# A two-layer kernel on one core: seven half-size sums on GpSimd, new landing places for x1, and another order in the second span

## What is computed

```python
def _L0_cond_ref(x, language_ids, W, Wr, A, B):
    base = jnp.einsum('btd,od->bto', x, W)
    logits = jnp.einsum('btd,ed->bte', x, Wr)          # 8 experts
    logits = logits + one_hot(language_ids) * 5.0
    topw, topi = jax.lax.top_k(logits, 2)
    weights = jax.nn.softmax(topw, axis=-1)
    gates = jnp.sum(one_hot(topi) * weights[..., None], axis=-2)
    h = jnp.einsum('btd,erd->bter', x, A)              # rank 16
    lora_out = jnp.einsum('bter,bte,eor->bto', h, gates, B)
    return base + 2.0 * lora_out

x = x + _L0_cond_ref(x, itok_B_0_7, L0_cond_W, L0_cond_Wr, L0_cond_A, L0_cond_B)
x = x + jnp.einsum('bsi,boi->bso', x, L1_cond_weight[itok_B_0_15])
```

## Time and profile before

| | us |
|---|---|
| median of 3 runs | 419.42 |
| lowest and highest | 417.97, 420.1 |
| the profiled execution | 418.74 |
| its span, first to last instruction | 416.7 |
| TensorE busy | 398.2 (96%) |
| VectorE busy | 315.4 (76%) |
| ScalarE busy | 170.9 (41%) |
| GpSimd busy | 56.6 (14%) |

### The profile page before, as it was taken

How to read it: one execution, slowest core, us unless ns; L and a number is a source line. 1 busy time by engine, 2 the same in 40 slices (tenths; PEclk the granted TensorE clock), 3 DMA queues, 4 the chain that set the end, 5 groups by cost and what they waited for, 6 DMA issues and landing times.

```text
span 416.7 us, 5965 instructions
## 1 busy us (share of the span) xinstructions
PE 398.2 (96%) x1920; PEld 333.2 (80%) x1920; DVE 315.4 (76%) x412; ACT 170.9 (41%) x231; POOL 56.6 (14%) x80
## 2 busy tenths in 40 slices
PE   8999989899999989999999997999998999999996
PEld 8989868688889868788888885878786887878784
DVE  2899999997454148929887489979797979899700
ACT  2342242664220141434353255555455564555511
POOL 1010100000000000000100025241231415142000
PEclk9999999999999999999999999999999999999999
DMA  8977510133476200007693999999999999999231
GB/s 189 218 212 194 152 53 0 51 102 101 127 216 207 57 0 2 1 1 204 138 302 106 329 232 263 282 257 293 280 263 281 254 304 258 284 264 295 62 102 50
DMA packets 78578, 72.79 MB, mean 175 GB/s; under 512 B 7091, under 2 KB 77267, under 8 KB 77523
## 3 DMA queue, kind: packets, MB, share of 16 engines
q1 hardware_dynamic: 51584, 47.21, 44.6%
q10 hardware_dynamic: 26962, 25.21, 19.4%
HBM read 55.61 MB, written 16.78 MB: 174 GB/s over the span
## 4 chain that ended last, share of the span: by engine, by line
PE 39%; DVE 33%; issue 14%; ACT 4%; DMA 4%; SPq 3%; ACTq 1%; POOL 1%; DVEq 0%
PE banks L1058 8%; PE banks L1060 8%; PE banks L1059 8%; DVE weights L612 7%; DVE weights_f L606 5%; DVE tokens L596 4%; DVE turned_w L612 4%; PE banks L1051 4%; SPq L371 3%; PE banks L1155 3%; PE banks L1156 3%; PE banks L1157 3%; DVE weights L462 2%; ACT tokens L916 2%; DVE turned_w_f L450 2%
## 5 line engine op out<-in xcount | busy, mean ns | idle before, releaser
L1058 PE MATMUL banks<-ring,weights 128*128 128x512 f32 x192 | 75.4, 393 | 5.2 <-DVE weights L462 1.7
L418 POOL TENSOR_TENSOR raw<-raw,ident 128x128 f32<-128x128 f32 x50 | 38.2, 764 | 269.2 <-DMA raw<-in_L_cond_weight_dram 230.1
L1155 PE MATMUL banks<-weights,tokens 128*128 128x512 f32 x176 | 68.9, 392 | 3.1 <-DVE tokens L596 3.1
L1156 PE MATMUL banks<-weights,tokens 128*128 128x512 f32 x176 | 68.5, 389 | 0.0
L1157 PE MATMUL banks<-weights,tokens 128*128 128x512 f32 x176 | 68.5, 389 | 0.0
L926 ACT ACTIVATE weights<-weights_f 128x1024 fp32r<-128x1024 f32 x44 | 46.6, 1062 | 52.9 <-DVE weights_f L606 51.2
L606 DVE STREAM_TRANSPOSE weights_f<-raw 128x1024 f32<-128x1024 f32 x42 | 51.7, 1232 | 1.4 <-POOL raw L418 0.8
L612 DVE TENSOR_TENSOR weights<-weights_f,weights 128x1024 fp32r<-128x1024 f32 x44 | 52.1, 1186 | 0.4 <-ACT weights L926 0.4
L1060 PE MATMUL banks<-ring,turned_w 128*128 128x512 f32 x128 | 49.8, 389 | 0.0
L1059 PE MATMUL banks<-tokens,weights 128*128 128x512 f32 x128 | 49.8, 389 | 0.0
L1058 PEld LDWEIGHTS banks<-ring,weights 128*128 128x128 f32 x192 | 36.0, 188 | 14.2 <-issue 3.2
(11 more groups left out here) (109 smaller groups left out, 626.6 us busy)
## 6 DMA issues: line engine op xcount, KB each, us to landing
raw<-in_L_cond_weight_dram SPq DMA_DIRECT2D x168, 128.0 KB, 3.6
ring_f<-in_L_cond_weight_dram SPq DMA_DIRECT2D x88, 128.0 KB, 6.2
raw<-in_x_dram SPq DMA_DIRECT2D x64, 128.0 KB, 3.3
x_kept<-stage ACTq DMA_DIRECT2D x32, 256.0 KB, 4.2
tokens_f<-x_kept ACTq DMA_DIRECT2D x8, 1024.0 KB, 8.3
out_dram<-sums ACTq DMA_DIRECT2D x32, 256.0 KB, 5.1
raw<-in_L_cond_W_dram SPq DMA_DIRECT2D x32, 128.0 KB, 3.0
raw<-in_L_cond_A_dram SPq DMA_DIRECT2D x4, 128.0 KB, 2.9
```

The source lines that it names most:

```text
L418: nc.gpsimd.tensor_tensor(spot, spot, ident[:].rearrange("p (q j) -> p q j", q=Q), ALU.add)\
L1058: nc.tensor.matmul(ps, u_hi, x_hi, start=first and k == 0, stop=False, skip_group_check=True)
L1155: nc.tensor.matmul(l1_bank(o), x_hi, w_hi, start=m == 0, stop=False)
L1156: nc.tensor.matmul(l1_bank(o), x_hi, w_lo, start=False, stop=False)
```

## The change

- In the first span the four T1, the first three S4 and the four S1 move from VectorE to GpSimd's list, between and behind its `add_ones`. T1(t) for t > 0 waits for T2(t - 1), S4(r) for S2(r), S1 for the end of the gates. VectorE makes S4(3) itself, after three S4 of GpSimd.
- In the second span `copy_h` and `exponentials` come ahead of the high parts for product 2 on ScalarE, and the gates and T3 ahead of its low parts on VectorE.
- In both spans TensorE turns the gated h after two k steps of product 7, before after three.
- x1 of rows 2 and up lands in `stage` (even rows) and `sums2` (odd rows). Row 3's load stands behind `high_w1(8)`, row 2's behind output 0, row r + 3's behind the first output of row r for r of 1 to 4; `x1_high(row + 2)` stands behind a row's last output, and `x1_low(row)` from row 2 on behind `low_w1` when n % 8 is 2. Row 1's stay.

The diff, with most of the unchanged lines around it cut:

```diff
@@ -351,6 +351,12 @@
+        def x1_landed(row):
+            if row < 2:
+                return x1_place(row, 1, tokens_f)
+            return stage[:] if row % 2 == 0 else sums2[:].rearrange("p (s a) f -> p s (a f)", s=2)
         def x1_part(row, low):
@@ -420,8 +426,40 @@
                 add_ones(("w", m))
+            def make_t1(t):
+                pool.wait_ge(featured, featured_at(0, 0, t) + 1)
+                if t == 0:
+                    pool.wait_ge(lo_done, PIECE_AT["wt", HM - 1] + 1)
+                else:
+                    pool.wait_ge(t2_done, t)
+                pool.wait_ge(transposed, TURN_AT[x_item(0, 1, t)] + 1)
+                nc.gpsimd.tensor_tensor(half_x(0, t, 0), half_x(1, t, 0), half_x(0, t, 0), ALU.subtract)\
+                    .then_inc(t1_done, 1)
+            def make_s4(r):
+                pool.wait_ge(s2_done, r + 1)
+                a12 = quarter_w(3, r)
+                nc.gpsimd.tensor_tensor(a12, a12, s2_sum(r), ALU.subtract).then_inc(s4_done, 1)
+            def make_s1(r):
+                pool.wait_ge(gate_steps, GATE_STEPS)
+                a21, a22 = quarter_w(5, r), quarter_w(4, r)
+                nc.gpsimd.tensor_tensor(a21, a21, a22, ALU.add).then_inc(s1_done, 1)
+            make_t1(0)
+            make_t1(1)
+            add_ones(("w", HM))
+            make_t1(2)
+            add_ones(("w", HM + 1))
+            make_t1(3)
+            add_ones(("w", HM + 2))
+            make_s4(0)
+            add_ones(("w", HM + 3))
+            make_s4(1)
+            make_s4(2)
             for r in range(HM):
-                add_ones(("w", HM + r))
+                make_s1(r)
             for n in range(NW1):
@@ -501,12 +539,6 @@
                     .then_inc(bd_summed, 1)
-
-            def make_s1(r):
-                dve.wait_ge(s3_done, r + 1)
-                dve.wait_ge(s2_done, r + 1)
-                a21, a22 = quarter_w(5, r), quarter_w(4, r)
-                nc.vector.tensor_tensor(a21, a21, a22, ALU.add).then_inc(s1_done, 1)
@@ -593,7 +625,7 @@
                     dve.wait_ge(x1_hi_done, 2 * row + j + 1)
-                    nc.vector.tensor_tensor(x1_place(row, 1)[:, j], x1_place(row, 1, tokens_f)[:, j],
+                    nc.vector.tensor_tensor(x1_place(row, 1)[:, j], x1_landed(row)[:, j],
                                             x1_place(row, 0)[:, j].bitcast(F32), ALU.subtract).then_inc(x1_ready, 1)
@@ -641,18 +673,14 @@
             low(("wt", 3))
-            make_t1(0, 0)
             turn(x_item(0, 1, 1))
             make_t2(0, 0)
-            make_t1(0, 1)
             turn(x_item(0, 1, 2))
             make_t2(0, 1)
-            make_t1(0, 2)
             turn(x_item(0, 1, 3))
             make_t2(0, 2)
-            make_t1(0, 3)
             turn(("w", 4))
@@ -676,22 +704,16 @@
             lows("u", 7)
-            for r in range(HM):
-                make_s4(r)
+            dve.wait_ge(s4_done, 3)
+            make_s4(3)
             lows("x", 0, 7)
             make_gates(0)
-            add_p1(0, 0)
-            add_p1(0, 1)
+            for r in range(HM):
+                add_p1(0, r)
             turn(("b",))
-            make_s1(0)
             low(("b",))
-            add_p1(0, 2)
-            add_p1(0, 3)
-            make_s1(1)
-            make_s1(2)
             gT_low(0)
-            make_s1(3)
@@ -747,24 +769,21 @@
             low(("x", 1, 1, 3))
-            lows("x", 1, 2)
             for t in range(XT):
                 make_t1(1, t)
+            make_gates(1)
+            for t in range(XT):
+                make_t3(1, t)
+            lows("x", 1, 2)
             for k in range(HM):
             low(("x", 1, 6, 3))
-            for t in range(XT):
-                make_t3(1, t)
             for r in range(HM):
                 add_p1(1, r)
-            low(("x", 1, 7, 0))
-            make_gates(1)
-            low(("x", 1, 7, 1))
-            low(("x", 1, 7, 2))
-            low(("x", 1, 7, 3))
+            lows("x", 1, 7)
             gT_low(1)
@@ -776,7 +795,9 @@
                 low_w1(n - 1)
-                if n % M == 5:
+                if n == M + 5:
+                    x1_low(1)
+                elif n > M + 5 and n % M == 2:
                     x1_low(n // M)
@@ -903,17 +924,21 @@
                     act.wait_ge(steps, product_end(1, 3))
-                else:
-                    act.wait_ge(l1_ready, (row - 1) * 2 * TT)
+                elif row == 3:
+                    act.wait_ge(summed_up, added_at(1, "12", HM - 1) + 1)
+                elif row >= 4:
+                    act.wait_ge(x1_ready, 2 * (row - 1))
                 for slot in range(KEPT):
-                    act.wait_ge(kept[slot], (HM if row < NB // 2 else 2 * HM) * 16)
-                act.dma_start(x1_place(row, 1, tokens_f).rearrange("p s f -> p (s f)"),
+                    act.wait_ge(kept[slot], (HM if row in (0, 1, 3) else 2 * HM) * 16)
+                act.dma_start(x1_landed(row).rearrange("p s f -> p (s f)"),
                               x1_kept[row].rearrange("p m t -> p (m t)")).then_inc(x1_loaded[row % 2], 16)
                 act.wait_ge(x1_loaded[row % 2], (row // 2 + 1) * 16)
+                if row >= 2:
+                    act.wait_ge(l1_ready, (row - 1) * 2 * TT)
                 for j in range(2):
-                    nc.scalar.activation(x1_place(row, 0)[:, j], x1_place(row, 1, tokens_f)[:, j],
+                    nc.scalar.activation(x1_place(row, 0)[:, j], x1_landed(row)[:, j],
                                          ACT.Copy).then_inc(x1_hi_done, 1)
@@ -1000,17 +1025,14 @@
             keep_all(0, "12")
-            highs("x", 1, 2)
             copy_h(1, 0)
             copy_h(1, 1)
+            exponentials(1)
+            highs("x", 1, 2)
             for r in range(HM):
             highs("x", 1, 6)
-            high(("x", 1, 7, 0))
-            exponentials(1)
-            high(("x", 1, 7, 1))
-            high(("x", 1, 7, 2))
-            high(("x", 1, 7, 3))
+            highs("x", 1, 7)
             for r in range(HM):
@@ -1018,6 +1040,7 @@
             high_w1(8)
+            load_x1(3)
             high_w1(9)
@@ -1025,10 +1048,14 @@
                 row, last = o // (2 * TT), o % (2 * TT)
-                if last == 1 and row + 1 < NB:
-                    x1_high(row + 1)
-                if last == 2 * TT - 1 and row + 2 < NB:
-                    load_x1(row + 2)
+                if o == 0:
+                    load_x1(2)
+                elif o == 1:
+                    x1_high(1)
+                elif last == 0 and row + 3 < NB:
+                    load_x1(row + 3)
+                elif last == 2 * TT - 1 and row + 2 < NB:
+                    x1_high(row + 2)
             for s in range(OUTS):
@@ -1105,9 +1132,9 @@
                 product(s, 6, lambda r: pe.wait_ge(p1_copied, HM * s + r + 1), False, main_bank)
-                product(s, 7, lambda r: pe.wait_ge(u2_copied, HM * s + r + 1), False, main_bank, range(HM - 1))
+                product(s, 7, lambda r: pe.wait_ge(u2_copied, HM * s + r + 1), False, main_bank, range(2))
                 turn_gated(s)
-                product(s, 7, None, False, main_bank, range(HM - 1, HM))
+                product(s, 7, None, False, main_bank, range(2, HM))
                 pe.wait_ge(gT_done, s + 1)
```

## The result

The changed kernel takes **414.31 us** (median of 4 runs, 413.56 to 414.8), the kernel before 419.36 beside it (4 runs); ratio 0.988, 95% interval 0.985 to 0.991. The forecast was 411.6, with a range of 407.3 to 416.6. The profiled execution took 414.6 us, its span is 412.8.

The account below looks back on a forecast made before the run. TensorE, busy 96% of 416.7 us, was taken as the bound, so only its idle time could be won. Spans -4.0, rows 2 to 7 -6.9, row 1 +3.6 sum to -7.3: 411.4 from 418.74, stated as 411.6, range 407.3 to 416.6.

Parts of the forecast that it names:

- product 6 later: First span: T1 saved on VectorE are given back as waiting, so product 6 starts 0.7 us later.
- the spans' four other waits: Both spans: TensorE's waits for gT_low, quarter 11's first addition, copy_h and copies of U2 go; -4.7 us.
- row 1's wait: Second layer, row 1: early x1 loads in row 0 delay W1 tiles 11 to 13; +3.6 us, ends 0 and +8.
- rows 2 to 7: Second layer: x1's high part made a row earlier lets VectorE catch up; all six waits go, -6.9 us.
- T1 was put at 1.4 us: First span: one 128x512 sum on GpSimd takes 1.4 us, between 0.46 and 1.84.
- The rival that these sums grow to over 2.4 us: First span: GpSimd's sums hold VectorE's second operand, product 6 about 11 us later, 423 in all; chance 0.07.
- the forecast 41.9: First span: T1(3) stands behind the ones of W piece 5, so T2(3) starts near 41.9 instead of 41.20.
- forecast a wait of 5 to 6.5 us: Sign of being right: TensorE waits 5 to 6.5 us at the start of row 1.
- its times for tiles 11 and 13, 245.0 and 249.6: Row 0: row 3's x1 load costs 4.8 us of W1 traffic, so tiles 11 and 13 land at 245.0 and 249.6.
- that it would be idle in every later row: Second layer, sign of being right: VectorE stands idle in each row after row 1.
- The rival that the weights' stream sets the rows: Rows 2 to 4: W1 stream sets them, or second load hits row 1; +2 to +5, 413.6 to 416.6; chance 0.20.
- 0.27 us: Amount added to each TensorE wait's idle time, taken from row 1's start, as its full cost.

Follow-up runs that it names:

- with the load moved away: Changed kernel with row 3's x1 load moved from behind high_w1(8) to behind row 0's last output; 411.0 us, ratio 0.979.
- the version with x1 early: Changed kernel with T1(2), T1(3) ahead of the ones, row 3's load behind row 0's last output, x1_high(1), x1_low(1) behind tile 9; 408.2 us.
- the ten with 48 fillers: Ten executions of the changed kernel with 48 unused identity matmuls on TensorE ahead of row 1's wait; median 416.8 us.

## Why the prediction was right, and where its sum was short

| term | predicted | measured |
|---|---|---|
| product 6 later | +0.7 | +1.06 (55.00 to 56.06) |
| clock behind product 6 | not in the sum | +1.6 |
| the spans' four other waits | -4.7 | -5.0 |
| row 1's wait | +3.6 | +3.3 |
| clock behind row 1 | not in the sum | +2.1 |
| rows 2 to 7 | -6.9 | -6.9 |

Measured is between the two profiled executions. The spans' term is what is left when the first two are taken from row 0's start, 226.72 instead of 229.00. That of rows 2 to 7 is 132.68 us from row 1's start to row 7's (254.44 to 387.12) against 137.48 before, -4.8, without the 2.1 of the clock. From -2.3, +3.3 and -4.8 follow -3.8, and the spans differ by 3.9.

**GpSimd's sums.** T1 was put at 1.4 us and took 1.27 to 1.30; beside a VectorE step with two operands S4 took 1.68, against 1.30 beside a transpose. In reverse, VectorE's low part and T2 beside T1(3) and the ones behind it took 1.06 and 0.94, where 0.65 and 0.69 is usual. This is the lock between a VectorE step with two SBUF inputs and a GpSimd instruction that reads SBUF, as the Trainium skill's "SBUF — State Buffer", section "Who interferes with whom", states it, and these rows agree. The rival that these sums grow to over 2.4 us is out. That T1(2) and T1(3) would stand behind the ones was foreseen, and T2(3) at 41.95, 0.75 us later than before, is the forecast 41.9 almost exactly. The other 0.3 us up to product 6 are lost behind it, where T2(3) took 0.94 us instead of 0.68.

**The first span behind product 6 and the second span.** The steps came within a microsecond of what was written, and all four waits went. gT_low ran from 77.26 to 78.48 and was done before lora, at 80.43; the four S1 ran from 70.74 to 75.79.

**Row 1.** The mechanism and the size were right: forecast a wait of 5 to 6.5 us, measured 5.80. The working has two faults. The load cost the stream 3.2 us and not 4.8. And the prediction took its times for tiles 11 and 13, 245.0 and 249.6, from a kernel whose spans were not yet shorter, while its sum has row 1's delay behind the spans' gain: with the load moved away tile 13 landed at 242.72, 2.0 us earlier than before, with the spans. So tile 13 landed at 245.98, not 249.6, and VectorE turned it at 247.48, not 250.1. By the prediction's own times a TensorE 4 us ahead would have waited some 10 us; the forecast of 5 to 6.5 comes from the 3.6 of the sum. The rest is ScalarE's: the high part of tile 13, an output and two halves of x1's high part follow one another from 248.75 to 252.9, and x1_low(1) stands 2.20 us waiting for it:

```profile
250.94 2.00 ACT L941 ACTIVATE tokens<-tokens_f 128x1024 fp32r<-128x1024 f32 x2 [0.65 <-ACT sums L962]
252.03 2.36 DVE L628 TENSOR_TENSOR tokens<-tokens_f,tokens 128x1024 fp32r<-128x1024 f32 x2 [2.20 <-ACT tokens L941]
```

From tile 13's landing to row 1's start it is 8.46 us (245.98 to 254.44), before 8.67 (244.76 to 253.43). The wait is this chain against a TensorE that arrives 2.3 us earlier and a tile that arrives 1.2 us later, 3.2 for the load less 2.0 for the spans.

**Rows 2 to 7.** All six waits went, as forecast, and rows 2 to 6 take 21.76 us each. Their cause was the one named: VectorE's own waits behind row 1's start, first before, then now (total us, times, longest):

```profile
DVE tokens L596 <- ACT tokens L916: 13.1, 6, 2.2
```

```profile
DVE weights_f L638 <- POOL raw L424: 3.0, 4, 1.9
DVE weights_f L638 <- POOL ring_f L424: 1.9, 3, 0.9
```

The wait for ScalarE's high part of x1 is gone, and VectorE waits 4.9 us for tiles instead, which TensorE doesn't feel. In rows 2 to 5 VectorE was busy for 19.50 to 21.40 us of 21.76; that it would be idle in every later row did not hold in row 6, where it was busy throughout and still in time. (The 1.4 us of waits for tiles that the prediction took from the page were those of 42 of the 64 tiles; the other 22 had 5.3 us, but none of it behind row 1's start.) The rival that the weights' stream sets the rows did not come here, since TensorE came late to row 1. With row 1 started at 254.44 the tiles cost nothing later, nor at 251.38 with the load moved; at 248.22 they cost a wait of 1.1 us, at 245.1, with no wait at row 1, 4.0 to 4.3. So the limit was real, and it takes most of what is won by repairing row 1 once product 6 is repaired.

**What was missing.** The sum priced a wait at its idle time and 0.27 us, from a row in which the clock held. It had no term for the clock, though it made one wait longer by 3.3 us and another by over 1. Those 1.6 + 2.1 us, with small differences of the other terms, are the whole way from 411.4 to 414.6. The range held them only by what it kept for the weights' stream: that the measured time lies inside it is luck to that extent.

## What to carry to other kernels

Price a wait of the engine at 97% in two parts: its idle time, and what its clock loses afterwards. Where an edit makes one wait longer and six shorter, look at the longer one first, in the spacing of the matmuls behind it, since a row of waits doesn't show it. And when work moves to an engine that also handles arrivals, put it ahead of the steps that wait for loads: 3 us here for the order of two lines.

## What the hardware showed that was not expected

**In these profiles the clock falls after idle times as short as 2.2 us, but not after each.** At product 6 the matmuls went to 0.43 us apart after 2.21, 2.46, 2.48 and 2.88 us of idle, at row 1 after 2.30, 2.38, 2.44, 2.64 and each of 5.2 to 5.8. It did not after any wait of up to 2.16 us, nor after 2.50 us at row 1 of the kernel before and 2.82 at row 3 of the version with x1 early. The length alone doesn't decide it. What else does stays open: 2.44 and 2.50 at row 1 have the same matmuls just before and behind them, and one and the same kernel loses the clock in some executions and keeps it in others, as the ten with 48 fillers show. One profile therefore doesn't tell whether a kernel with waits near 2.5 us pays for them; the mean clocks of many executions do. Nor is the moment fixed: after the 2.48 us the first matmul was slow already (0.56 to the next), after the 2.88 us the sixth (57.28). The fall cost 1.5 to 2.6 us each time.

**A small matmul is not cheap.** One of 128 columns in float32 took 0.22 us and left two records, against 0.227 us for 512 columns in the format of the large products.
